# Attention with the divide moved to the output: scores shifted by their row maximum on ScalarE out of PSUM, turned, then exponentiated; the plain block first in the loop

## The chip, the cores and the metric

The kernel runs on one core of a Trainium2 chip. The metric is the device time of one execution in microseconds (us); before the change the median of three runs is 200.62 us. The core's engines are TensorE (PE, with its weight load PEld), VectorE (DVE), ScalarE (ACT), GpSimd (POOL) and SyncE (SP), each with its own instruction queue; they meet at semaphores. All data here is f32.

## The reference, cut to what matters

```python
x = x + conv2d_depthwise(x, 51x51 weights)          # [16, 32, 16, 16]
t = tokens(x)                                       # 16 batches, 256 tokens, 32 channels
# attention over LayerNorm(t), with a mask that also depends on data
scores = where(mask, einsum('bid,bjd->bij', Q, K) * scale, -inf)
w = nan_to_num(softmax(scores, axis=-1))            # 16 x 256 x 256
out = einsum('bij,bjd->bid', w, V) @ Wo + bo        # added to t, then normed per channel group
# 33 steps; in each, the first token's largest channel picks the weights (op) and two flags
def step(h, p):
    op = argmax(h[0, 0, :19])
    attn = softmax(einsum('bqd,bkd->bqk', h @ wq[op], h @ wk[op]) * scale)
    y = einsum('bqk,bkd->bqd', attn, h @ wv[op]) @ wo[op]
    h = where(am[op], y, h)
    z = relu(h @ w1[op] + b1[op]) @ w2[op] + b2[op]
    h = where(fm[op], z, h)
```

Steps whose two flags are both off change nothing and are skipped. With this case's data three steps are left: one with the feed-forward block alone (kind 1, "plain block") and two with attention and feed-forward (kind 3).

## The kernel before, in words

The state is held as hT: 128 partitions (4 batches of 32 channels), 4 groups g of 4 batches, 256 tokens. One run goes: convolution and LayerNorm (to 44 us of the profile); projections and the LIF sweeps on DVE that give the mask (`sweeps`, L1216); the first, masked attention (`attention_pe`, `attention_act`, `attention_dve` with `masked`); a norm (`centred`, `variance`, `scale` on PE, `squared`, `deviation` on ACT, `inverted`, `placed`, `normed` on DVE and POOL); and a loop that each engine runs for itself, on registers read from a table with the picked op (`next_step`). In the loop of before the body is: block A for kinds 2 and 3 (attention), then blocks for kind 1, kind 3 and kind 2. The first pass of this data is of kind 1, so each engine jumps over block A.

Attention goes over 16 batches b, two halves of 128 query rows each. Per batch:

1. PE: scores, 2 products of 128 x 256 (L555). The queries lie in `qz`, where all rows but the batch's 32 are zero, so that a product over all 128 rows gives one batch; 16 copies of 32 x 256 fill it (L981 on ACT; L1050 on ACT and L1412 on DVE in the loop).
2. DVE: the row maximum (L1256; with the mask L1253, which also writes the masked scores to `minus`).
3. ACT: the exponential with the maximum as bias, and the row sum (L905, two of 128 x 256).
4. DVE: the reciprocal of the two sums per row (L1264); POOL: `prob` scaled by it (L448, twice).
5. PE: `turn_pe`, 4 transposes to PSUM (L528); DVE: copy to `probT` (L1269).
6. After every fourth batch PE weighs the values, `weigh_pe` (L542, 8 products of 32 columns), and ACT (in the masked one DVE) drains 128 x 256.

PE's order is fixed: three batches of scores ahead, then per batch scores(b+3), turn(b) and, behind every fourth, the weighing. The last three turns stand in the next block. The feed-forward of kind 3 (`ffn`): token 0's hidden column (L829) and the first batch of hidden products (L813), token 0's row (L834), the last weighing into bank 5 (L843), the second batch of hidden products (it needs group 3 of hT), the outputs (L859), products of the next weights (L772). DVE picks the next op (`pick_op`: L1168, L1158 to L1162); on it SP issues the next weights' DMAs (L419, L420).

Of the kernel before, what the change touches and what calls it, by code (L numbers as in the profile page):

```python
# [6 lines left out]
BF16 = mybir.dt.bfloat16  # L7
# [82 lines left out]
def build(nc, d):  # L90
    with ExitStack() as ctx:
# [11 lines left out]
        def part(t, n):  # L103
# [9 lines left out]
        onesb = sb("onesb", [B, P], BF16)  # L113
        maskc = sb("maskc", [P, NH, S])
# [25 lines left out]
        seen = sb("seen", [1, 1])  # L140

# [12 lines left out]
        qz = sb("qz", [P, B, S])  # L154
        v = sb("v", [P, NH, B, C])
        NPB, NTB = 3, 2 * GB
        prob = [sb(f"prob{i}", [P, NH, S]) for i in range(NPB)]
        relu = big[:, 0:GB * NG * S].rearrange("p (q g s) -> p q g s", q=GB, g=NG)
        probT = [big[:, (GB * NG + NH * i) * S:(GB * NG + NH * (i + 1)) * S].rearrange("p (h s) -> p h s", h=NH)
                 for i in range(NTB)]  # L160
        nmax = sb("nmax", [P, B, NH])
        esum = sb("esum", [P, B, NH])
        einv = sb("einv", [P, B, NH])
        negm = sb("negm", [P, NH, S])
        minus = [sb(f"minus{i}", [P, NH, S]) for i in range(3)]
# [40 lines left out]
        wa = sb("wa", [C, NWA + HID])  # L206
        wf = sb("wf", [HID, C + 2])
        w1r = sb("w1r", [P, HID])
        wfs = sb("wfs", [HID, C + 2])
# [31 lines left out]
        s_S, s_nm, s_P, s_ri, s_Pn, s_T, s_PT = (sem(n) for n in (  # L241
            "scores_in_psum", "row_max_ready", "exponentials_ready", "row_sums_inverted", "probs_ready",
            "probsT_in_psum", "probsT_copied"))
# [4 lines left out]
        s_w1p = sem("first_ffn_rows_placed")  # L248
# [11 lines left out]
        RING = 3  # L260
        SCORES = (0, 1, 4)
        AHEAD = len(SCORES)
# [13 lines left out]
        ATTY = "AAAA"  # L276
        RESY = "DDDD"
        CENTREB = (1, 4, 5, 6)
        VARB = (0, 2, 5, 3)
        LPRE = "ADAD" + "ADAD"  # L280
# [15 lines left out]
        MAIN = B - GB + 1  # L296
        LATTF = LPRE + ATTY[:NG - 1] + FF[:GB] + "A" + FF[GB:]
        K_HF = len(LPRE) + NG - 1
        HBANK = ((0, 1, 4, 2), (5, 6, 3, 7))
        TOKEN0 = bank[7]  # L300
        ZBANK = (1, 4, 2, 5)
        PBANK = (6, 7)
# [4 lines left out]
        class Tasks:  # L307

            def __init__(self, owners, at=0, a=0, d=0):  # L310
                self.owners, self.at, self.a, self.d = owners, at, a, d

            def bank(self, k):
                return bank[8 - RING + k % RING]

# [18 lines left out]
        st = Tasks(STATIC)  # L334
# [104 lines left out]
        def attention_pool(pool, reg_att=None):  # L439
            for b in range(B):  # L440
                if reg_att is None:
                    pool.wait_ge(s_ri, b + 1)
                else:
                    att = pool.snap(reg_att) + 1
                    pool.wait_ge(s_ri, att)
                    pool.reg_alu(reg_att, reg_att, 1, ALU.add)
# [1095 lines left out]
```

## Time and the profile before

| | us |
|---|---|
| median of 3 runs | 200.62 |
| lowest, highest | 198.45, 200.82 |
| span of the profiled execution | 199.1 |
| first products of the two attention rounds start at | 112.73, 153.90 |
| last output stored | 199.1 |

The span runs from the first to the last instruction of the profiled execution. Times below are from its start. The row "PEclk" or the column of that name is the clock granted to TensorE as a share of full speed.

### The profile page before, as it was taken

Reading aid. Unit: us, or ns where it says so; the run is one execution under the profiler, and the core shown is the slowest. Engines: PE = TensorE matmul, PEld = TensorE weight load, DVE = VectorE, ACT = ScalarE, POOL = GpSimd, SP = SyncE. Lnnn points to the kernel's source line nnn. Section 1 sums busy time; section 2 is a strip of 40 time slices with the busy share of each in tenths; the row PEclk is TensorE's granted clock in tenths of the full one; section 3 lists DMA queues with packets and bytes.
Section 4 is the critical chain, followed back from the end, with each engine's and each line's share of the span. In section 5 each row is a group of like instructions: output and inputs, shape, how many; then the busy total and the mean of one; then the engine's idle time right before and its main releaser. Section 6 shows DMA issues by size and latency. Waiting matters only on the chain.

```text
span 199.1 us, 4262 instructions
## 1 busy us (share of the span) xinstructions
PE 166.5 (84%) x1255; PEld 112.6 (57%) x1256; DVE 134.3 (67%) x382; ACT 111.3 (56%) x324; POOL 64.1 (32%) x153
## 2 busy tenths in 40 slices
PE   7999989693898998879929679999867699998770
PEld 5779744241685776647412468776533587775320
DVE  1364578819938889896506388898756689789481
ACT  3464511429767656555405568675655877664670
POOL 8940000100061555453600005655510036556300
PEclk9999999969579999999966999999999999999997
DMA  5900000000000000000000100000000000000003
GB/s 158 315 3 0 3 0 3 0 3 2 0 2 0 2 0 3 0 0 18 3 7 2 20 0 0 0 0 0 0 0 15 0 0 0 0 0 0 0 0 110
DMA packets 3020, 3.33 MB, mean 17 GB/s; under 512 B 889, under 2 KB 2361, under 8 KB 3002
## 3 DMA queue, kind: packets, MB, share of 16 engines
q1 hardware_dynamic: 2858, 2.85, 4.8%
q10 hardware_dynamic: 144, 0.25, 0.4%
q8 instruction: 9, 0.15, 0.3%
q14 instruction: 9, 0.07, 0.1%
HBM read 2.58 MB, written 0.53 MB: 16 GB/s over the span
## 4 chain that ended last, share of the span: by engine, by line
PE 60%; DVE 16%; issue 9%; ACT 8%; POOL 2%; DVEq 1%; ACTq 1%; POOLq 0%
PE bank L555 17%; PE bank L528 8%; PE bank L615 5%; PE bank L542 5%; ACT qz L981 4%; PE bank L679 4%; PE bank L813 3%; PE bank L512 3%; DVE big L1269 3%; PE bank L633 3%; PE bank L600 2%; POOL prob L448 2%; PE bank L694 2%; ACT qz L1050 1%; ACT prob L905 1%
## 5 line engine op out<-in xcount | busy, mean ns | idle before, releaser
L448 POOL TENSOR_SCALAR prob<-prob,einv 128x256 f32<-128x256 f32 x96 | 44.7, 478 | 60.6 <-DVE einv L1264 60.4
L1269 DVE COPY big<-bank 128x512 f32<-128x512 f32 x48 | 32.9, 685 | 5.7 <-PE bank L528 5.7
L905 ACT ACTIVATE prob<-bank,nmax 128x256 f32<-128x256 f32 x64 | 29.8, 473 | 11.6 <-DVE nmax L1256 11.6
L528 PE MATMUL bank<-ident,prob 128*128 128x128 f32 x192 | 30.2, 280 | 6.5 <-POOL prob L448 6.4
L555 PE MATMUL bank<-hT,qz 128*128 128x256 f32 x128 | 32.7, 383 | 0.0
L528 PEld LDWEIGHTS bank<-ident,prob 128*128 128x128 f32 x192 | 21.4, 140 | 18.2 <-POOL prob L448 14.1
L1256 DVE TENSOR_REDUCE nmax<-bank 128x2 f32<-128x512 f32 x32 | 21.6, 687 | 4.8 <-PE bank L555 4.6
L555 PEld LDWEIGHTS bank<-hT,qz 128*128 128x128 f32 x128 | 22.3, 190 | 3.6 <-issue 1.6
L905 ACT ACTIVATE prob<-minus,nmax 128x256 f32<-128x256 f32 x32 | 16.0, 500 | 8.9 <-DVE nmax L1253 7.9
L555 PE MATMUL bank<-kt,qz 128*128 128x256 f32 x64 | 16.5, 386 | 0.9 <-ACT prob L905 0.9
L905 ACT ACTIVATION_READ_ACCUMULATOR prob<-bank,nmax 128x1 f32 x64 | 12.9, 202 | 0.0
L1253 DVE CUSTOM_DVE_ANT_0 minus<-bank,negm 128x256 f32<-128x256 f32 x32 | 11.9, 415 | 1.5 <-PE bank L555 1.5
L555 PEld LDWEIGHTS bank<-kt,qz 128*128 128x128 f32 x64 | 11.1, 190 | 3.2 <-ACT prob L905 1.4
L931 ACT ACTIVATE big<-bank 128x512 f32<-128x512 f32 x14 | 8.2, 598 | 8.2 <-PE bank L615 8.2
L615 PEld LDWEIGHTS bank<-ident,filt 128*128 128x128 f32 x96 | 10.9, 144 | 1.0 <-issue 0.7
L615 PE MATMUL bank<-ident,filt 128*128 128x128 f32 x96 | 11.4, 276 | 0.0
L1106 DVE COPY big<-bank 128x512 f32<-128x512 f32 x10 | 6.8, 686 | 6.6 <-PE bank L615 6.6
L1069 ACT ACTIVATE big<-bank,wfs 128x512 f32<-128x512 f32 x12 | 7.6, 683 | 6.5 <-PE bank L813 6.5
L542 PE MATMUL bank<-big,v 128*32 128x256 f32 x160 | 10.7, 385 | 0.0
L813 PE MATMUL bank<-hT,w1r 32*128 32x512 f32 x48 | 9.7, 800 | 1.1 <-ACT hT L1065 1.1
L1412 DVE COPY qz<-bank 32x256 f32<-32x256 f32 x16 | 6.7, 420 | 5.0 <-PE bank L512 4.9
L595 PE MATMUL bank<-constf,ident 128*128 128x512 bf16 x36 | 8.8, 380 | 0.7 <-DVE xc L1178 0.6
(173 smaller groups left out, 256.8 us busy)
## 6 DMA issues: line engine op xcount, KB each, us to landing
xrev<-xrev_dram SPq DMA_DIRECT2D x1, 512.0 KB, 4.5
xin<-xtok_dram SPq DMA_DIRECT2D x1, 512.0 KB, 5.0
out_dram<-outT SPq DMA_DIRECT2D x2, 256.0 KB, 3.3
maskc<-maskc_dram SPq DMA_DIRECT2D x1, 256.0 KB, 4.8
kx<-kx_dram ACTq DMA_DIRECT2D x1, 248.0 KB, 3.1
wx<-wx_dram SPq DMA_DIRECT2D x1, 216.0 KB, 2.9
constf<-constf_dram SPq DMA_DIRECT2D x1, 186.0 KB, 4.6
wa<-wa_dram SPq DMA_DIRECT2D x3, 56.0 KB, 1.8
```

The costliest lines, as they stand in the source:

```text
L448: last = nc.gpsimd.tensor_scalar(prob[b % NPB][:, ih, :], prob[b % NPB][:, ih, :], einv[:, b, ih:ih + 1], 1.0, ALU.mult, ALU.mult)
L528: mm = pe.transpose(bank[2 + b % 2][:, jh * S + ih * P:jh * S + (ih + 1) * P], prob[b % NPB][:, ih, jh * P:(jh + 1) * P], ident)
L542: mm = pe.matmul(t.bank(k0 + g)[q * C:(q + 1) * C, 0:S], v[:, jh, b, :], probT[b % NTB][:, jh, :], start=(jh == 0), stop=(jh == NH - 1), t ...
L555: mm = pe.matmul(bank[SCORES[b % AHEAD]][:, ih * S:(ih + 1) * S], qz[:, b, ih * P:(ih + 1) * P], keys[:, b // GB, :], start=True, stop=True)
L595: pe.matmul(into, ident[:, 0:P // 2].bitcast(BF16), constf[:, 0:2 * P].bitcast(BF16), start=True, stop=True)
L615: mm = pe.transpose(bank[TBANK[n]][:, u * P:(u + 1) * P], flat(filt[:, ck, a0:a0 + YH, :]), ident)
L813: pe.matmul(bank[HBANK[gp][q]][:, :], w1r[rows, :], flat(hT[rows, 2 * gp:2 * gp + 2, :]), start=True, stop=True, tile_position=(q * C, 0)) ...
L905: e = nc.scalar.activation(prob[b % NPB][:, ih, :], scores, ACT.Exp, bias=nmax[:, b, ih:ih + 1], scale=-1.0 if masked else 1.0, accum_out= ...
L931: nc.scalar.activation(dst, src, ACT.Copy).then_inc(s_toepA, 1)
L1253: m = nc.vector.tensor_tensor_reduce(minus[b % AHEAD][:, ih, :], bank[SCORES[b % AHEAD]][:, ih * S:(ih + 1) * S], negm[:, ih, :], -1.0, -F ...
L1256: m = nc.vector.tensor_reduce(nmax[:, b, :], bank[SCORES[b % AHEAD]][:, :].rearrange("p (h j) -> p h j", h=NH), AX.X, ALU.max, negate=True)
L1269: nc.vector.tensor_copy(flat(probT[b % NTB]), bank[2 + b % 2][:, :]).then_inc(s_PT, 1)
```

## The change: what it does

- **Scores.** `qz` and its zero fill go. The queries are copied as they are, 4 copies of 128 x 256 to `qT` (all on ACT). A batch's scores are products over its own 32 rows (`score_pe`, a row position of the array for each of 4 batches); two batches are issued together, 4 in the front. Score banks are 4, `b % 4`.
- **Exponentials.** In the loop ACT writes scores minus maximum to `sh` (two of 128 x 256, out of PSUM), PE turns that (banks 4 and 5), and ACT takes the exponential of 128 x 512 out of PSUM into `probT`, now 16 tiles. ACT's list is shift(b+4), then exponential(b). In the masked attention DVE writes the masked scores to `sh`, POOL subtracts the maximum, ACT takes the exponential. No row sums on ACT, no reciprocal and no POOL work per batch in the loop, no copy by DVE.
- **Division.** `weigh_pe` gets 8 more products with ones (`onesc`), which leave each batch's sums beside its weighed values; in the masked one also a small product (`tiny`). DVE takes the reciprocal of 128 x 256 and multiplies (`normed_output`), 4 times per attention. In the loop the first two stand in DVE's list behind the row maxima of batches 10 and 14.
- **PE's order.** Per pair n: scores of 2n+4 and 2n+5, turn(2n), for even n the weighing of the group before, turn(2n+1).
- **Masked tail.** All turns now stand ahead; POOL adds the residual of groups 0 and 1, DVE that of 2 and 3 behind its own division.
- **Feed-forward of kind 3.** Outputs of groups 0 and 1 come ahead of the second hidden batch; the latter waits for DVE's division of group 3; DVE's first two relus come ahead of `pick_op`.
- **Loop.** Kind 1 comes first, and its pass falls through to attention. The exponentials' table is asked for once ahead of the loop, not in block A. `w1` moves from the `wa` load to `wf`, repeated for 4 rows groups, and one copy (POOL in the loop) places it.
- **PSUM.** Ring of 2 banks where it was 3, plus two banks for the weighed values; other banks are renumbered.

```diff
+        def score_pe(pe, b, h, keys):
+            g, rows, at_row = strip(b)
+            mm = pe.matmul(bank[b % 4][:, h * S:(h + 1) * S], qT[rows, g, h * P:(h + 1) * P], keys[rows, g, :],
+                           start=True, stop=True, tile_position=at_row)
...
         def weigh_pe(pe, base, t, k0, g):
+            t.drained(pe, k0 + max(g - 1, 0))
...
+            wait(pe, s_P, base, GB * (g + 1))
+            out = bank[YBANKS[g % 2]]
             for jh in range(NH):
                 for q in range(GB):
                     b = g * GB + q
+                    pe.matmul(out[q * C:(q + 1) * C, 0:S], v[:, jh, b, :], probT[b][:, jh, :],
+                              start=(jh == 0), stop=(jh == NH - 1), tile_position=(0, q * C))
+            if t is st:
+                pe.matmul(out[:, S:2 * S], onesq[:, :], tiny[:, :], start=True, stop=False)
+            for jh in range(NH):
+                for q in range(GB):
+                    mm = pe.matmul(out[q * C:(q + 1) * C, S:2 * S], onesc[:, :], probT[g * GB + q][:, jh, :],
+                                   start=t is not st and jh == 0, stop=(jh == NH - 1), tile_position=(0, q * C))
...
+            for n in range(B // 2):
+                if n + 2 < B // 2:
+                    wait(pe, s_nm if masked else s_sh, base, 2 * n + 2)
+                    scores_pe(pe, (2 * n + 4, 2 * n + 5), keys)
+                turn_pe(pe, base, 2 * n)
+                if n % 2 == 0 and n:
+                    weigh_pe(pe, base, t, k0, n // 2 - 1)
+                turn_pe(pe, base, 2 * n + 1)
...
+            def shift_scores(b):
+                wait(act, s_nm, base, b + 1)
+                if b >= NSH:
+                    wait(act, s_T, base, b - NSH + 1)
+                for ih in range(NH):
+                    e = nc.scalar.activation(sh[b % NSH][:, ih, :], bank[b % 4][:, ih * S:(ih + 1) * S], ACT.Identity,
+                                             bias=nmax[:, b, ih:ih + 1])
+                e.then_inc(s_sh, 1)
...
             for b in range(B):
+                if not masked and b + 4 < B:
+                    shift_scores(b + 4)
+                wait(act, s_T, base, b + 1)
+                nc.scalar.activation(flat(probT[b]), bank[4 + b % 2][:, :], ACT.Exp, scale=-1.0 if masked else 1.0).then_inc(s_P, 1)
...
+            def normed_output(t, k, g, to):
+                t.filled(dve, k)
+                link(nc.vector.reciprocal(sinv[:, g, :], bank[YBANKS[g % 2]][:, S:2 * S]))
+                return nc.vector.tensor_tensor(to[:, g, :], bank[YBANKS[g % 2]][:, 0:S], sinv[:, g, :], ALU.mult)
...
+            def attention_dve(base, masked, output, early=()):
+                for b in range(B):
                     row_max(base, b, masked)
+                    if b == 3:
+                        for e in early:
+                            e()
+                    if b in (10, 14):
+                        output((b - 10) // GB)
...
+                def ahead():
+                    product_pe(pe, t, 0, bda[:, :], hT[:, 0, :], S)
+                    product_pe(pe, t, 1, bda[:, :], hT[:, 1, :], S)
+                    t.drained(pe, 1)
+                    scores_pe(pe, (0, 1, 2, 3), hT)
+                    product_pe(pe, t, 2, bda[:, :], hT[:, 2, :], S)
+                    product_pe(pe, t, 3, bda[:, :], hT[:, 3, :], S)
                     for g in range(NG):
                         values(t, NG + g, hT, g, bdv[:, :])
...
+                    token0(r)
+                    hidden(r, 0)
+                    token0_row()
+                    weigh_pe(pe, att, t, len(LPRE), NG - 1)
+                    k = K_HF + GB + 1
+                    t.drained(pe, k - 1)
+                    outputs(t, k, (0, 1))
+                    t.drained(pe, k)
+                    hidden(r, 1)
```

## Rows read from the trace of the kernel before

**Rows 1.** Busy time by stretch: start:end, length, each engine's busy us, PEclk, DMA.

```profile
62.00:91.00 29.00, 25.65 (x173) 17.77 (x171) 25.16 (x115) 17.77 (x66) 14.88 (x32) 1.00 0.00 1
99.50:112.70 13.20, 7.75 (x58) 3.31 (x58) 4.89 (x13) 4.12 (x9) 0.09 (x1) 0.74 0.05 11
121.00:146.00 25.00, 23.01 (x167) 16.65 (x165) 20.48 (x49) 16.71 (x63) 14.60 (x32) 1.00 0.00 0
```

**Rows 2.** Chain that ended last, a loop batch: start, us, scores then turn.

```profile
163.64 0.86 PE bank L555 x4
164.50 0.44 PE bank L528 x4
```

**Rows 3.** Timeline, masked attention, VectorE: start, us, engine, line, operation.

```profile
68.01 0.16 DVE L1263 TENSOR_SCALAR esum<-esum 128x2 f32<-128x2 f32 x1
...
69.56 0.16 DVE L1263 TENSOR_SCALAR esum<-esum 128x2 f32<-128x2 f32 x1
```

**Rows 4.** Groups by line and shape: xcount, busy us, mean ns, idle before.

```profile
L542 PE MATMUL bank<-big,v 128*32 128x256 f32 x160 | 10.7, 385 | 0.0
L1264 DVE RECIPROCAL einv<-esum 128x2 f32<-128x2 f32 x48 | 7.7, 160 | 0.8
L1302 DVE RECIPROCAL invg<-devg 32x32 f32<-32x32 f32 x4 | 1.2, 326 | 1.2 <-ACT devg L1011 1.2
```

**Rows 5.** Timeline, second round's start and feed-forward: instructions back to back.

```profile
147.37 1.26 ACT L1069 ACTIVATE big<-bank,wfs 128x512 f32<-128x512 f32 x2 [0.71 <-PE bank L813]
148.54 1.41 DVE L1441 TENSOR_SCALAR big<-bank,wfs 128x512 f32<-128x512 f32 x2
148.96 1.14 PE L813 MATMUL bank<-hT,w1r 32*128 32x512 f32 x8 [0.55 <-ACT hT L1065]
151.27 0.84 ACT L1075 ACTIVATE hT<-bank,wfs 128x256 f32<-128x256 f32 x2
159.52 1.89 DVE L1256 TENSOR_REDUCE nmax<-bank 128x2 f32<-128x512 f32 x3
```

**Rows 6.** Timeline, VectorE at the start of the masked attention.

```profile
60.02 0.42 DVE L1243 TENSOR_SCALAR spm<-bank 128x256 f32<-128x256 f32 x1 [2.38 <-PE bank L512]
61.21 0.42 DVE L1253 CUSTOM_DVE_ANT_0 minus<-bank,negm 128x256 f32<-128x256 f32 x1
```

**Rows 7.** Timeline, TensorE during the projections: the same two records twice.

```profile
48.05 0.70 PE L512 MATMUL bank<-xt,bdk 128*128 128x256 f32 x2 [1.22 <-ACT qz L981]
49.98 1.22 PE L512 MATMUL bank<-xt,bdk 128*128 128x256 f32 x2 [1.23 <-ACT qz L981]
```

**Rows 8.** Timeline, from the last masked turn to the plain block's first product.

```profile
91.01 0.66 PE L528 MATMUL bank<-ident,prob 128*128 128x128 f32 x4 [0.16 <-POOL prob L448]
94.81 0.70 PE L722 MATMUL bank<-outT,centre 128*128 128x256 f32 x2
99.44 0.42 DVE L1309 TENSOR_TENSOR hT<-bank,hT 128x256 f32<-128x256 f32 x1 [0.79 <-PE bank L736]
103.33 0.34 PE L829 MATMUL bank<-hT,w1r 32*128 32x1 f32 x1 [3.92 <-issue]
```

**Rows 9.** Timeline, plain block: op picked, next weights' DMA, next round's first product.

```profile
106.13 0.18 DVE L1168 COPY row<-bank 1x32 f32<-1x32 f32 x1 [6.27 <-PE bank L835]
107.00 0.14 DVE L1162 TENSOR_SCALAR opi<-top 1x1 int32<-1x1 f32 x1
108.84 0.32 SPq L419 DMA_DIRECT2D wa<-wa_dram  x1
112.73 1.53 PE L512 MATMUL bank<-hT,bda 128*128 128x256 f32 x6 [1.14 <-DVE bdv L1209]
```

**Rows 10.** Timeline, second round: first product of attention, of the feed-forward, row copy.

```profile
153.90 1.56 PE L512 MATMUL bank<-hT,bda 128*128 128x256 f32 x6 [0.57 <-DVE bdv L1209]
187.27 0.27 PE L829 MATMUL bank<-hT,w1r 32*128 32x1 f32 x1
...
188.86 0.18 DVE L1168 COPY row<-bank 1x32 f32<-1x32 f32 x1 [0.79 <-PE bank L835]
```

More of the change, by code:

```diff
@@ L470, in _, with residual, residuals @@
                     nc.gpsimd.tensor_tensor(vg, vg, rep(bvo[:, :], GB), ALU.add).then_inc(s_vb, 1)
-            attention_pool(pool)
+            def residual(g):
+                wait(pool, s_dd, 0, count("D", STATIC[:K_ATT + g + 1]))
+                wait(pool, s_da, 0, count("A", STATIC[:K_ATT]))
+                nc.gpsimd.tensor_tensor(outT[:, g, :], outT[:, g, :], yn[:, g, :], ALU.add).then_inc(s_resP, 1)
+            def residuals(b):
+                if b >= 12 and (b - 12) % 3 == 0:
+                    residual((b - 12) // 3)
+            masked_pool(pool, residuals)
             reg_att = pool.alloc_register("pool_att")
@@ L749, in _ @@
             variance(0)
-            wait(pe, s_PT, 0, B - 1)
             variance(1)
@@ new lines, in hidden, with outputs @@
+                def hidden(r, gp):
+                    for q in range(GB):
+                        rows = slice(q * C, (q + 1) * C)
+                        if (gp, q) == (1, GB - 1):
+                            pe.wait_ge(s_rowc, r)
+                        pe.matmul(bank[HBANK[gp][q]][:, :], w1r[rows, :], flat(hT[rows, 2 * gp:2 * gp + 2, :]),
+                                  start=True, stop=True, tile_position=(q * C, 0)).then_inc(s_task, 1)
+                def outputs(t, k, ns):
+                    for i, n in enumerate(ns):
+                        for q in range(GB):
+                            mm = pe.matmul(bank[ZBANK[n]][q * C:(q + 1) * C, 0:S], w2s, relu[:, q, n, :],
+                                           start=True, stop=True, tile_position=(0, q * C))
+                        mm.then_inc(s_task, 1)
@@ new lines, in outputs @@
+                def outputs(t, k, ns):
+                    for i, n in enumerate(ns):
+                        t.filled(act, k + i)
+                        nc.scalar.activation(hT[:, n, :], bank[ZBANK[n]][:, 0:S], ACT.Identity, bias=b2s).then_inc(s_da, 1)
+                with act.If(kind == 1):
+                    t = Tasks(FF, act.snap(reg_task))
+                    token0(r)
+                    hidden(t, 0, 0)
+                    hidden(t, GB, 1)
+                    outputs(t, 2 * GB, (0, 1, 2))
```

600 lines of the change are left out of this document (268 added, 332 removed).

## The prediction, made before the changed kernel was run

> **What bounds the kernel now.** I read the busy time by stretch first. In the loop's attention (121 to 146 us) TensorE is busy 23.0 of 25.0 us, VectorE 20.5, ScalarE 16.7, at full clock; in the masked one (62 to 91) TensorE 25.7 and VectorE 25.2 of 29 [rows 1]. The chain of work says which of the two it is. In the loop it alternates scores, 0.86, and turn, 0.44, without a gap: 1.30 a batch [rows 2], and a weighing about 1.0 more every fourth (16 records in two passes of the four column strips). In the masked attention VectorE comes round every 1.55 us (68.01 to 69.56) with no idle time in between [rows 3]: it is the bound there. The third place is a hole: hT is ready at 99.44 + 0.42 = 99.86, TensorE starts the plain block at 103.33 after 3.92 us of "issue" [rows 8], and the stretch behind it runs at a mean clock of 0.74 [rows 1].
>
> **Prices.** Turn 0.44; a batch's scores 0.86 over all rows [rows 2]. Hidden products use row strips already: four of 512 columns in 1.14 us, against 4 x 0.86 if they ran one by one (512 columns are twice 256, so 0.86 each) [rows 2, 5]. So strips overlap, and a pair of batches costs 0.86 (0.43 each); if two strips did not overlap, 1.72. Weighing about 1.0 today: 160 records are 10 weighings of 16, four strips at a time [rows 4]; with the ones it doubles, about 2.1. ScalarE: two of 128x512 end in 1.26, two of 128x256 in 0.84, and a single lasts 0.68 and 0.47, so in a row they cost 0.58 and 0.37 [rows 5]. Shift plus exponential: 2 x 0.37 + 0.58 = 1.32 a batch. Row maximum 0.60 in a row, 0.69 alone [rows 5]. POOL's subtraction: as its scaling today, 14.88 / 32 = 0.465, twice a batch [rows 1].
>
> The one operation that is new in kind is VectorE's reciprocal of 128x256. Two elements take 160 ns and 32 take 326 [rows 4], 5.5 ns an element, so 256 take 0.15 + 256 x 0.0055 = 1.55 us. Below that bound stands a plain pass of 256 at 0.42 [rows 6]; above, I allow 2.0. I take 1.55, as both rows are reciprocals. With the multiply 2.0 us a group. The two rows show less than this, and no run here has the length of 256 yet.
>
> **To the masked attention.** `qz`'s copies go, but the mask comes from VectorE's sweeps, which don't change: they end 2.38 us before L1243 at 60.02, which waited for TensorE (busy with scores) [rows 6]. That wait goes; row maxima start near 59.3. The first turn is held by TensorE itself: it now idles some 4 us before the mask, and its clock should be half, as for the record pair of 0.70 that took 1.22 [rows 7]. Transposes of the residual and the spare products then end near 62.4, first turn 63.3.
>
> **Masked attention.** VectorE drops to 0.69 a batch, ScalarE to 0.58, POOL to 0.93; TensorE is the bound: 6 score pairs x 0.86 + 16 turns x 0.44 + 3 weighings x 2.15 = 18.7. Last turn ends at 82.0 instead of 91.67 [rows 8]: -9.7.
>
> **The norm behind it gives much back.** Before, 91.67 to 99.86: 8.2 us. After, from the last turn X: token 0's product and its pick 1.4; division 2 and its residual 2.45 (X+3.85); meanwhile the last weighing and two variances (X+4.7); `centred(2)` 0.6; ScalarE's squares and copies of group 2 and two deviations, which stand behind it, 1.3; two inversions 0.6 (X+7.2); only then division 3, 2.45 (X+9.65). From `centred(3)` on it is as before, 94.81 to 99.86 = 5.05 [rows 8]. X+14.7 = 96.7 instead of 99.86: -3.2.
>
> **Plain block.** Before, 99.86 to 112.73 [rows 8, 9] = 12.9: 3.5 hole, 2.8 to the row copy (at full clock it is 188.86 - 187.27 = 1.6 [rows 10], so 1.2 is slow clock), 2.7 to the DMA, 3.9 to the next product [rows 9]. With the block first, nothing is jumped over; first product to first product then is 9.4 - 1.2 = 8.2: 96.7 + 8.2 = 104.9, -7.8 in all. This needs TensorE's clock up. In the norm it is busy about 0.9 us between X+5 and X+9, less than the share that went before the fall in rows 7 (0.70 in each 1.92); so I let it fall there: +1.5 (spare products, variance, row). -6.3.
>
> **A round's attention,** from its first product (0). Scores of four batches end at 2.2, row maximum 2.9. ScalarE's list mixes 4 shifts with 4 copies, and TensorE's value products wait for these (ring of 2): scores(4) end at 8.35, and exponential 3 at 14.4. From here in groups of four, E3 = end of exponential 3: weighing 2.1 (it waits for E3), turn 5 0.45, scores(10) 1.0, row maximum 0.7: shift 10 at E3+4.4. ScalarE alone would be there at E3+2.6. Division 0 then stands before row maximum 11: +2.0+0.7, shift 11 at E3+7.15; exponential 7 behind it ends at E3+8.5. Before, four batches cost 4 x 1.30 + 1.05 = 6.3. The next group is the same (row maximum 15 behind division 1): E11 = 31.4. The last weighing in the loop 2.1 and turn 13, exponentials 13 and 14: feed-forward at 35.5, against 187.27 - 153.90 = 33.4 [rows 10]. +2.1.
>
> **A round's feed-forward.** Before: second hidden batch 2.9 behind the first (148.96 against 112.73 + 33.4 = 146.1), next product 4.9 behind it [rows 5, 9, 10]. After: VectorE's relu pair 1.4 [rows 5] from +1.3, pick 1.0 (106.13 to 107.14) [rows 9], division 3 from 3.7 to 5.75: second batch at +5.8. +2.9; in the last round +2.5, as the first outputs are added up by then.
>
> **Sum.** -6.3 + (2.1 + 2.9) + (2.1 + 2.5) = +3.3 us. The profiled span is 199.1 and goes to 202.4; the median of runs lies 1.5 above that span, so I add the sum to the median: 203.9. Costed at nothing: `qz`'s zero fill on POOL (TensorE's chain hides it), the table load (ScalarE waits at its place anyhow), the bigger `wf` load and its one copy by POOL (a dozen batches of cover; bare it would be about 0.5).
>
> **Rivals.**
> - *Rounds at ScalarE's pace* (faster): if the weighing and divisions slip into gaps, a batch costs 1.32, 21.1 for 16 where 25 stood: -3.9 instead of +2.1 in each round: -6.3 - 2 x 3.9 + 5.4 = -8.7, 191.9. For it: every engine has room on average. Against: the lists above put the weighing in front of the turns ScalarE needs. 0.08.
> - *The reciprocal costs like a plain pass* (faster): 0.42 instead of 1.55 at the 8 places where it is on the path (2 in the norm, 3 a round): 203.9 - 9.0 = 194.9. It decides from about 0.65 us down. Against: rows 4. 0.17.
> - *TensorE's clock falls inside the rounds* (slower): between exponentials 9 and 11 it does one turn in 4 us. At half clock the weighing, three turns and the hidden batch behind cost 2.8 more, twice: 209.5. For it: rows 7. Against: before, no such gap fell in a round (clock 1.00 [rows 1]). 0.25.
> - *The hole moves*: the second pass now jumps over the plain block; a hole of 3.9 there gives 207.8. Before, the second pass's jump back cost nothing like it (idle 0.57 before 153.90 [rows 10]). 0.05. The Trainium skill ("Runtime: NRT & Kernel Launch", Instruction fetch mechanics) says a taken branch beyond the fetched pages stalls; the trace agrees for 103.33, 3.92 us, and not for 153.90.
>
> **How the numbers follow.** The worked sum has 0.45, with its own range 200 to 207.5 (score pairs, weighing 1.9 to 2.3, reciprocal up to 2.0). The range takes in both a cheap reciprocal and a fallen clock: 194.5 to 209.5. A difference under 2% (4 us) can't be told from none here. Faster by that: the two faster rivals, 0.25. Within: most of the main case, 0.34. Slower: the two slower rivals and a third of the main case, up to 0.41.
>
> **What would show it.** Reciprocal 128x256 at 1.55; masked last turn near 82; hT near 97, the plain block's first product right behind it with no issue gap; round's first product to feed-forward 35.5 with ScalarE waiting on row maxima 10, 11, 14, 15; second hidden batch 5.8 behind the first. It would be wrong if the reciprocal were short, if the weighing were under 1.6, or if TensorE's clock stayed low.

## The result, and the profile after

The changed kernel takes 229.43 us (median of 4 runs, 226.39 to 229.82) against 200.5: 1.141 times the time of before, interval 1.129 to 1.153. Slower was the likeliest sign in the prediction, but 229.4 lies 20 us above the top of its range (194.5 to 209.5). Some runs of every kernel are a few per cent longer, at a lower granted clock: ratios and their 95% intervals are of the fast runs alone, while medians and ranges are of all runs.

The marks of the prediction, in us from the start of each profiled execution. "Predicted" are its numbers on the way to a span of 202.4, its 1.5 us of slow clock in the norm included from the round's first product on. e2, e6 and e4 are experiments described below.

| | before | predicted | after | e2 | e6 | e4 |
|---|---|---|---|---|---|---|
| last masked turn ends | 91.67 | 82.0 | 98.71 | 86.88 | 84.10 | 90.52 |
| plain block's first product | 103.33 | 96.7 | 115.44 | 102.78 | 100.07 | 98.78 |
| round 1's first product | 112.73 | 106.4 | 124.19 | 111.81 | 107.99 | 106.84 |
| round 2's first product | 153.90 | 152.6 | 174.49 | 160.88 | 154.07 | 148.07 |
| end | 199.1 | 202.4 | 227.5 | 214.8 | 203.7 | 192.6 |

After misses by 17.8 us at round 1's first product, by 4.1 more in round 1 (50.3 where 46.2 was predicted) and by 3.2 in round 2 (53.0 against 49.8). Together 25.1, all of the distance from 202.4 to 227.5.

Busy time by stretch of after, columns as in [rows 1]: the masked attention, the norm, the later part of round 1's attention.

```profile
61.40:98.70 37.30, 30.87 (x218) 16.59 (x217) 14.88 (x64) 9.22 (x16) 37.26 (x34) 0.78 0.00 1
98.70:115.70 17.00, 14.16 (x124) 8.35 (x127) 9.26 (x22) 6.52 (x15) 2.50 (x5) 0.70 0.03 8
146.00:158.00 12.00, 7.68 (x68) 4.65 (x72) 4.10 (x6) 6.56 (x16) 0.21 (x1) 0.80 0.01 2
```

In the masked attention GpSimd is busy 37.26 of 37.30 us, where it had 14.88 of 29 before [rows 1]. The chain of work of after says that nothing else counts there (start, us, what):

```profile
61.43 22.68 POOL shifted L448 x21
84.11 0.85 issue
84.96 5.00 POOL shifted L448 x5
...
91.27 6.73 POOL shifted L448 x6
98.00 0.04 issue
98.05 0.66 PE bank L562 x4
```

The groups of after by line and shape, columns as in [rows 4]: the subtraction, the exponential, the reciprocal, and the two halves of the weighing.

```profile
L448 POOL TENSOR_SCALAR shifted<-shifted,nmax 128x256 f32<-128x256 f32 x32 | 35.9, 1142 | 6.4 <-DVE nmax L1314 6.4
L960 ACT ACTIVATE big<-bank 128x512 f32<-128x512 f32 x48 | 28.4, 605 | 40.2 <-PE bank L562 40.2
L1322 DVE RECIPROCAL sinv<-bank 128x256 f32<-128x256 f32 x12 | 20.9, 1745 | 10.1 <-PE bank L582 10.1
L576 PE MATMUL bank<-big,v 128*32 128x256 f32 x192 | 17.0, 484 | 8.7 <-ACT big L960 8.7
L582 PE MATMUL bank<-big,onesc 128*32 128x256 f32 x192 | 16.5, 470 | 0.0
```

A subtraction takes 1142 ns where the scaling on the same engine, with the same shape and the same name of instruction, took 465 ns in a row and 478 as a mean of single records. The weighing's records average 484 ns against 385 [rows 4], which is not a longer product but a lower clock. Round 1 shows where, in its chain of work:

```profile
142.72 1.76 DVE sinv L1322
...
144.88 0.66 DVE nmax L1317
...
146.29 0.61 ACT big L960
146.89 0.14 issue
147.03 1.94 PE bank L576 x16
148.97 1.36 PE bank L582 x16
...
152.61 1.76 DVE sinv L1322
...
156.92 1.94 PE bank L576 x16
158.85 1.53 PE bank L582 x16
```

The reciprocal stands ahead of the row maximum, and the shift and the exponential hang on that. TensorE has nothing in the meantime (2.09 us idle ahead of 147.03 and ahead of 156.92) and then weighs at half clock: the granted clock is 0.50 from 147 to 149 and from 156.9 to 159, and back at 1.00 by 150 and by 160.3. The weighing takes 1.94 + 1.36 and 1.94 + 1.53 us where the same work at full clock takes 1.07 + 0.86 (it did so at 138.50 in this trace). In round 2 the same gap stands ahead of the second and the third weighing, but only the third is slow (1.78 + 2.01 in the timeline, from 207.65). The second has full clock behind a gap as long:

```profile
199.12 1.07 PE L576 MATMUL bank<-big,v 128*32 128x256 f32 x16 [2.09 <-ACT big L960]
```

### The profile page after: what moved, and what is told of

Read it like the earlier page. It is cut to its first block, busy times and chain, and to the rows that moved or that the text cites. A ratio compares the mean times of both kernels' runs of the same rounds, so it can differ in the third digit from the quotient of the medians.

```text
span 227.5 us, 4254 instructions
## 1 busy us (share of the span) xinstructions
PE 178.8 (79%) x1443; PEld 108.1 (48%) x1447; DVE 114.7 (50%) x265; ACT 97.1 (43%) x211; POOL 54.2 (24%) x93
## 4 chain that ended last, share of the span: by engine, by line
PE 40%; DVE 22%; POOL 16%; ACT 9%; issue 9%; DVEq 1%; ACTq 0%; POOLq 0%
POOL shifted L448 15%; PE bank L630 5%; ACT shifted L945 5%; DVE sinv L1322 5%; PE bank L544 4%; PE bank L576 4%; PE bank L582 4%; DVE mem L1276 3%; PE bank L828 3%; ACT big L960 3%; PE bank L648 2%; DVE nmax L1317 2%; PE bank L562 2%; PE bank L835 2%; PE bank L615 2%
## 5 line engine op out<-in xcount | busy, mean ns | idle before, releaser
L960 ACT ACTIVATE big<-bank 128x512 f32<-128x512 f32 x48 | 28.4, 605 | 40.2 <-PE bank L562 40.2
L562 PE MATMUL bank<-ident,shifted 128*128 128x128 f32 x192 | 30.6, 292 | 11.2 <-POOL shifted L448 6.4
L448 POOL TENSOR_SCALAR shifted<-shifted,nmax 128x256 f32<-128x256 f32 x32 | 35.9, 1142 | 6.4 <-DVE nmax L1314 6.4
L945 ACT ACTIVATE shifted<-bank,nmax 128x256 f32<-128x256 f32 x64 | 27.4, 492 | 18.2 <-DVE nmax L1317 18.2
L562 PEld LDWEIGHTS bank<-ident,shifted 128*128 128x128 f32 x192 | 21.4, 147 | 25.3 <-POOL shifted L448 10.6
L1322 DVE RECIPROCAL sinv<-bank 128x256 f32<-128x256 f32 x12 | 20.9, 1745 | 10.1 <-PE bank L582 10.1
L1314 DVE CUSTOM_DVE_ANT_0 shifted<-bank,negm 128x256 f32<-128x256 f32 x32 | 11.6, 420 | 13.6 <-PE bank L544 13.5
L544 PE MATMUL bank<-hT,qT 32*128 32x256 f32 x128 | 16.8, 434 | 0.0
L582 PE MATMUL bank<-big,onesc 128*32 128x256 f32 x192 | 16.5, 470 | 0.0
L544 PEld LDWEIGHTS bank<-hT,qT 32*128 32x128 f32 x128 | 10.1, 201 | 3.8 <-issue 1.7
L980 ACT ACTIVATE big<-bank 128x512 f32<-128x512 f32 x14 | 8.3, 600 | 8.6 <-PE bank L630 8.6
L630 PE MATMUL bank<-ident,filt 128*128 128x128 f32 x96 | 11.8, 282 | 0.0
```

What stands on the lines that cost most here:

```text
L448: last = nc.gpsimd.tensor_scalar(sh[b % NSH][:, ih, :], sh[b % NSH][:, ih, :], nmax[:, b, ih:ih + 1], 1.0, ALU.subtract, ALU.mult)
L544: mm = pe.matmul(bank[b % 4][:, h * S:(h + 1) * S], qT[rows, g, h * P:(h + 1) * P], keys[rows, g, :], start=True, stop=True, tile_position ...
L562: mm = pe.transpose(bank[4 + b % 2][:, jh * S + ih * P:jh * S + (ih + 1) * P], sh[b % NSH][:, ih, jh * P:(jh + 1) * P], ident)
L582: mm = pe.matmul(out[q * C:(q + 1) * C, S:2 * S], onesc[:, :], probT[g * GB + q][:, jh, :], start=t is not st and jh == 0, stop=(jh == NH ...
L630: mm = pe.transpose(bank[TBANK[n]][:, u * P:(u + 1) * P], flat(filt[:, ck, a0:a0 + YH, :]), ident)
L945: e = nc.scalar.activation(sh[b % NSH][:, ih, :], bank[b % 4][:, ih * S:(ih + 1) * S], ACT.Identity, bias=nmax[:, b, ih:ih + 1])
```

## The experiments

In order of what they settle. Each ratio is to runs of before on the same chip. The experiments are spread over four chips, on which the median of before was 200.6 to 201.5, so a difference of 1 us between medians of two experiments means little. Where the text compares stages, it compares the profiled executions, one for each kernel.

### The price of the subtraction: e1_probe, e2_pool_ones, e5_pool_add

Theory A: GpSimd's price depends on the operation. Theory B: on the data (the masked scores hold -1e30). Theory C: GpSimd is slow for a reason in this stage. e1 puts seven instructions at the end of GpSimd's list:

```diff
+            nc.gpsimd.tensor_scalar(scr(0), x256, one, 1.0, ALU.mult, ALU.mult)
+            nc.gpsimd.tensor_scalar(scr(1), x256, one, 1.0, ALU.subtract, ALU.mult)
+            nc.gpsimd.tensor_scalar(scr(2), big30, one, 1.0, ALU.subtract, ALU.mult)
+            nc.gpsimd.tensor_scalar(scr(3), x256, one, 1.0, ALU.add, ALU.mult)
+            nc.gpsimd.tensor_scalar(scr(4), x256, one, 0.0, ALU.mult, ALU.add)
+            nc.gpsimd.tensor_tensor(scr(5), x256, one.broadcast_to([P, S]), ALU.subtract)
+            nc.gpsimd.tensor_tensor(scr(6), x256, one.broadcast_to([P, S]), ALU.mult)
```

> The changed kernel, and behind its loop seven operations of GpSimd on 128x256 f32: multiply-multiply, subtract-multiply (ordinary data, then data with -1e30), add-multiply, multiply-add, and two tensor-tensor forms (subtract, multiply). Their output is used nowhere. Theory A (the pair of operations sets the price): multiply-multiply 0.46 to 0.48 us, subtract-multiply 1.1 us on both data. Rival B (the data sets it): 0.47 on ordinary data and 1.1 on the masked one. Rival C (the place in the masked stage, shared with VectorE, sets it): all about 0.47 here.

The timeline of e1's GpSimd (start, us), in the order of the diff:

```profile
216.23 0.48 POOL L527 TENSOR_SCALAR probe<-xt,onesc 128x256 f32<-128x256 f32 x1 [20.15 <-issue]
216.69 1.15 POOL L528 TENSOR_SCALAR probe<-xt,onesc 128x256 f32<-128x256 f32 x1
217.81 1.15 POOL L529 TENSOR_SCALAR probe<-negm,onesc 128x256 f32<-128x256 f32 x1
218.93 0.48 POOL L530 TENSOR_SCALAR probe<-xt,onesc 128x256 f32<-128x256 f32 x1
219.38 0.48 POOL L531 TENSOR_SCALAR probe<-xt,onesc 128x256 f32<-128x256 f32 x1
219.82 1.05 POOL L532 TENSOR_TENSOR probe<-xt,onesc 128x256 f32<-128x256 f32 x1
220.83 0.61 POOL L533 TENSOR_TENSOR probe<-xt,onesc 128x256 f32<-128x256 f32 x1
```

With `subtract` 1.15, with any of `mult` and `add` 0.48, and the subtraction costs the same on both data. A holds; B and C fall. (e1 as a whole took 227.24 us in its one run.)

e2 replaces the subtraction with a multiply by ones, in place:

```diff
-  nmax[:, b, ih:ih + 1], 1.0, ALU.subtract, ALU.mult)
+  onesc[:, 0:1], 1.0, ALU.mult, ALU.mult)
```

> The changed kernel with GpSimd's subtraction of the row maximum in the masked attention replaced by a multiplication with ones (the same form as the kernel before has; the maximum is left out of these exponentials). If GpSimd's 1.14 us an operation set the masked attention, it falls to 0.47 and the last masked turn comes at about 83 us instead of 98.7, the time at 213 to 215 us. If the price is the place's and not the operation's, nothing changes.

215.98 us (214.05 to 219.25), ratio 1.076 (1.047 to 1.105). The last masked turn ends at 86.88 instead of 98.71, so the subtraction is worth 11.8 us. TensorE then bounds the stage (columns as in [rows 1]):

```profile
64.00:87.00 23.00, 22.32 (x214) 14.10 (x214) 12.89 (x52) 8.49 (x16) 13.67 (x29) 0.98 0.01 2
```

e5 keeps the mathematics: x times -1 plus the maximum, and +1 as the exponential's scale.

```diff
-  nmax[:, b, ih:ih + 1], 1.0, ALU.subtract, ALU.mult)
+  minusone[:, 0:1], nmax[:, b, ih:ih + 1], ALU.mult, ALU.add)
```

> The changed kernel with GpSimd's subtract-multiply written as multiply by -1, then add the maximum (the exponential's sign turned with it): the same results. The multiply-add form measured 0.482 us against 1.145. Expected 214 to 217 us, as with the ones (216.0), last masked turn near 87. Rival: the sign or the pointer in second place brings the slow price back, 229.

214.63 us (213.08 to 219.35), ratio 1.071 (1.057 to 1.084): two operands and another pair of operations are worth 14.8 us of median, 11.9 of it by the last masked turn (86.80). In place the form with two pointer operands takes a little more than the 0.48 of e1:

```profile
L449 POOL TENSOR_SCALAR shifted<-shifted,minusone,nmax 128x256 f32<-128x256 f32 x32 | 17.3, 555 | 12.3 <-DVE nmax L1316 12.3
```

The next kernels build on e5.

### The subtraction elsewhere: e3_masked_act

The masked attention gets the loop's list: ScalarE shifts b+4 (and turns the sign), then exponentiates b; GpSimd subtracts nothing.

```diff
-                if not masked and b + 4 < B:
+                if b + 4 < B:
                     shift_scores(b + 4)
```

> The changed kernel with that subtraction on ScalarE, as in the loop (same results). ScalarE then has 1.32 us a batch, and TensorE 1.4 to 1.5 with the weighing: last masked turn at 84 to 88 us, time 215 to 219 us. If GpSimd was not the bound, no change from 229.

225.82 us (225.77 to 226.21), ratio 1.132 (1.117 to 1.147): 7 us above the top of what was expected. The last masked turn ends at 96.74. The stage now has the loop's trouble: in e3 TensorE's weighings waited 13.3 us for ScalarE over the whole kernel, in after 8.7. In e3's masked attention the reciprocals start at 75.88 and 86.48, ahead of row maxima; TensorE then idles 2.19 and 2.18 us, and the products with ones behind take 1.94 and 1.93 us where 1.07 stood at 72.43.

So ScalarE's busy time, 21.1 of 35 us there, was not the limit; by the trace its shifts wait for row maxima behind a division. No run has e3 with the division moved.

### The division ahead of a row maximum: e6_divide_later, e7_weigh_later, e8_short_reciprocal

e6 is e5 with each division one row maximum later:

```diff
-                    if b in (10, 14):
-                        output((b - 10) // GB)
+                    if b in (11, 15):
+                        output((b - 11) // GB)
```

> The last kernel with VectorE's first two divisions behind the row maxima of batches 11 and 15 instead of 10 and 14. Theory (the division ahead of a row maximum stalls ScalarE's shift and with it the exponential that the weighing waits for): about 1.4 us less per division in the loop, four of them, 5 to 6 us less than without it, so 210 to 211. Rival (the next thing late is TensorE, and the stall moves to the second division or the weighing): under 2 us less.

203.44 us (202.72 to 205.55), ratio 1.016 (1.006 to 1.025): 11.2 less than e5 by medians, twice what was expected, for one exchange. Its chain of work in round 1:

```profile
122.34 1.07 PE bank L578 x16
123.41 0.86 PE bank L584 x16
...
126.56 0.68 DVE nmax L1319
127.24 1.68 DVE sinv L1324
...
128.94 0.44 DVE hT L1325
129.37 1.06 PE bank L578 x16
130.44 0.86 PE bank L584 x16
```

From weighing to weighing 7.03 us, where after has 8.53 (138.50 to 147.03) and then 9.89. The row maximum goes first, ScalarE works beside the reciprocal, and TensorE's clock is still up when the second weighing comes. The third, at 136.39, still has half clock for most of its length (1.45 and 2.01 us for its two halves in the timeline). The weighing's bank is now what it waits for, 0.59 us.

Not all of the 11.2 us is the exchange's. The two rounds take 46.1 + 49.6 = 95.7 us in e6 against 103.0 to 103.3 in e2, after and e7 (below), which have e5's place of the division: some 7.4 us. (e5 itself was profiled in its longest run, with 105.8.) The rest lies ahead of the rounds, where executions differ though the code that runs there is the same: the first masked turn starts at 62.67 in e6, 62.87 in e9 and 62.66 in e10, but at 65.37 in e5 and e8 and 65.46 in e2. In the first three the granted clock is 0.88 or 1.00 from 62 to 63 us, in the others 0.50.

e7 is e5 with the weighing behind both turns of its pair instead of between them:

```diff
-                if n % 2 == 0 and n:
-                    weigh_pe(pe, base, t, k0, n // 2 - 1)
                 turn_pe(pe, base, 2 * n + 1)
+                if n % 2 == 0 and n:
+                    weigh_pe(pe, base, t, k0, n // 2 - 1)
```

> The kernel with the add form, and each weighing behind turn(2n+1) instead of ahead of it. Theory: exponential 2n+1 no longer waits for the weighing, but the next pair's scores still do; 0.5 us less for each of the first two weighings and 2 us for the last one in each round: 4 to 6 us less than without it. Rival: TensorE has to do the weighing anyway before the scores that ScalarE waits for next, so only the last weighing counts: 2 to 3 us less.

215.16 us (214.76 to 215.54), ratio 1.077 (1.067 to 1.087): no gain over 214.63, where 4 to 6 us were expected. TensorE's wait for ScalarE moves from the weighing to the turns (12.3 us ahead of them in e7, 4.9 in e2). The weighing's place is not the cause.

e8 is e6 with the reciprocals of groups 1 to 3 over 32 columns:

```diff
-                link(nc.vector.reciprocal(sinv[:, g, :], bank[YBANKS[g % 2]][:, S:2 * S]))
+                m = S if g == 0 else C
+                link(nc.vector.reciprocal(sinv[:, g, 0:m], bank[YBANKS[g % 2]][:, S:S + m]))
```

> Add form and later divisions (203.4), and the reciprocals of groups 1 to 3 taken over 32 of the 256 columns (the rest of the divisors is left at 1: the division is left out for most tokens of these groups; group 0, from which the next step is picked, is whole). 0.33 us where 1.75 stood. If the reciprocal stands on the path in the norm (two) and ahead of the second hidden batch (one a round) and half of one ahead of the third weighing, 2.8 + 2 x 2.0 = 6.8 us less, 196 to 199. If it is hidden once the order is changed, 202 to 204.

202.21 us (200.62 to 204.72, 10 runs), ratio 1.010 (1.004 to 1.017), only 1.2 below e6, whose interval overlaps. In the profiled executions, which are among the longest of each kernel (204.61 and 205.55 us), the rounds are 3.7 and 1.0 us shorter (42.4 against 46.1, 48.6 against 49.6), where 4.0 was expected. In the norm, where 2.8 was expected, nothing comes back: from the last masked turn to the plain block's first product it is 15.91 us against 15.97. Division 3 is off the path there, or level with another: `centred(3)` starts 9.22 us behind the last turn in e8 and 9.46 in e6, though both reciprocals before it are 1.4 us shorter, because TensorE's spread and variance products, which wait for GpSimd's `invs`, end at about the same time. Round 1 of e8 begins 3.7 later (111.72 against 107.99): 2.7 of it stands at the last masked turn (86.80 against 84.10), from the later start above, and 1.1 comes in the plain block, where the granted clock from 100 to 108 us was 0.50 in e8 and 1.00 in e6. Whether the other nine runs lost the same, the traces don't say. The short reciprocal's group in e8 (the long one's mean there is 1749 ns):

```profile
L1326 DVE RECIPROCAL sinv<-bank 128x32 f32<-128x32 f32 x9 | 3.1, 344 | 8.4 <-PE bank L585 8.4
```

### TensorE's clock: e9_keep_clock, e10_later_and_clock

e9 is e5 with 8 spare products ahead of the waits of the weighings of groups 1 and 2 in the rounds; e10 has the same on e6.

```diff
             out = bank[YBANKS[g % 2]]
+            if t is not st and g in (1, 2):
+                for _ in range(8):
+                    pe.matmul(out, ident[:, 0:P // 2].bitcast(BF16), constf[:, 0:2 * P].bitcast(BF16), start=True, stop=True)
             wait(pe, s_P, base, GB * (g + 1))
```

> The kernel with the add form, and eight spare products (1.7 us at full clock, written into the bank that the weighing overwrites) ahead of the wait of the second and third weighing of each round, where TensorE idled 2.1 us. If the half clock behind these gaps costs 1.5 to 3 us a round, 3 to 5 us less, and the granted clock in the rounds 1.00. If the clock costs nothing there (other waits end last): no change, or 0.5 us more.

208.44 us (three of four runs at 208.4, one at 215.39), ratio 1.042 (1.029 to 1.055), 6.2 below e5 by medians; the clock of 120 to 148 us is 1.00 and the weighing's records take 384 ns:

```profile
120.00:148.00 28.00, 24.98 (x258) 14.87 (x258) 14.57 (x23) 17.30 (x39) 0.44 (x2) 1.00 0.01 2
L581 PE MATMUL bank<-big,v 128*32 128x256 f32 x192 | 12.9, 384 | 1.4 <-ACT big L965 1.4
```

More work for TensorE made the rounds faster: they take 47.3 + 51.1 = 98.4 us against 103.2 in e7 and 103.0 in e2. That is 4.6 to 4.8 us, some 2.4 a round, for the clock behind these gaps. The rest of the 6.2 lies ahead of the rounds, where e9 has no spare products. What falls later stays: from the first hidden batch of round 1 to round 2's first product it is 12.1 us in e9, as in after.

> Add form, later divisions, and the spare products ahead of the second and third weighing of each round. The gaps are shorter here (0.6 us of wait), so the spare products now cost time where there is no gap, and the clock fell only at the last one (records of 2.01 where 1.07 stood): 202 to 204, no gain. Rival: the clock still costs in each round, 200 to 201.

209.81 us (207.86 to 213.55), ratio 1.051 (1.033 to 1.070), 6 us above e6 and above the 202 to 204 expected. Where the gap is only 0.59 us long, the spare products themselves are what the weighing waits for: round 1's second weighing starts 22.4 us into the round instead of 21.4. The two repairs don't add up. But in the profiled executions the rounds are only 1.5 us longer than e6's (97.2 against 95.7), so most of the 6 us is not explained by the traces.

### The plain block first, by itself: e4_before_plain_first

Before, with nothing of the change but the order of the blocks in each engine's loop:

```diff
+                with pe.If(kind == 1):
+                    ffn(...)
+                # the step's code is read again
                 with pe.If(kind >= 2):
                     ...
-                with pe.If(kind == 1):
-                    ffn(...)
```

> The kernel before with one part of the change alone: the plain block first in the loop, falling through to attention. The 3.5 us hole ahead of 103.33 goes, and with it 1.2 us or more of half clock: 195 to 196.5 us. Rival: the hole moves to the second pass, which now jumps over the plain block: 199 to 201.

194.94 us (194.03 to 195.64), ratio 0.977 (0.960 to 0.993): the fastest of all kernels here, just under the 195 to 196.5 expected. The interval lies below 1, though it takes in gains of less than 2%. The timeline of TensorE from the end of the norm, where [rows 8] had 3.92 us of "issue":

```profile
98.78 0.24 PE L813 MATMUL bank<-hT,w1r 32*128 32x1 f32 x1 [0.52 <-issue]
```

The clock in the plain block is 1.00 (99 to 107 us) where it was 0.75 (103 to 113). No hole came up in the second pass, which jumps over the plain block.

### Scores by strip: e11_plain_first_strips, e12_strips_table, e13_strip_pairs, e14_turn_then_pair

e11 is e4 with `qT` and strip products, one batch at a time behind the first three, which are issued together; the attention is otherwise that of before. e12 also asks for the exponentials' table once, ahead of the loop.

```diff
-                    mm = pe.matmul(bank[SCORES[b % AHEAD]][:, ih * S:(ih + 1) * S], qz[:, b, ih * P:(ih + 1) * P],
-                                   keys[:, b // GB, :], start=True, stop=True)
+                    mm = pe.matmul(bank[SCORES[b % AHEAD]][:, ih * S:(ih + 1) * S], qT[rows, g, ih * P:(ih + 1) * P],
+                                   keys[rows, g, :], start=True, stop=True, tile_position=(q * C, 0))
```

> The kernel before with two parts of the change: plain block first, and queries copied whole with scores over each batch's own 32 rows (no zero-filled tile, three batches ahead issued together); softmax order, POOL scaling and copies as before. In each round 16 small copies fall to 4 (3.8 us between first product and scores falls to 1.8) and the first three batches' scores take 1.1 instead of 2.6: -3.5 a round. In the masked attention the mask no longer waits 2.4 us for TensorE: -2. From 194.9 to 185 to 187. Rival (a batch of 32 rows is not faster by itself, and a later engine takes the gain): 190 or more.

199.9 us (197.72 to 201.54, and one of the ten runs at 237.28), ratio 0.999 (0.992 to 1.006), 5 us slower than e4 and 13 above what was expected. TensorE's chain in the loop:

```profile
119.77 0.59 PE bank L527 x4
120.36 1.06 PE bank L559 x4
```

A batch takes 1.65 where it took 1.30 [rows 2]: scores 1.06 for 0.86, turn 0.59 for 0.44.

> The last one, and the exponentials' table asked for once ahead of the loop instead of in each attention block. In each round ScalarE's first query copy waited for 1.5 us of table load and dummy; with the copies short this is on the path: 0.8 to 1 us less a round, 183 to 185. Rival: a load is placed in the block anyhow, no change.

204.64 us (200.44 to 218.14, 11 runs), ratio 1.007 (1.000 to 1.015): no gain in time from the table's place, and some 20 above what was expected, mostly for the reason of e11. The load did leave the block. In round 1 this gives nothing, since in e11 the load (108.62 to 109.90) and its dummy end before ScalarE's first query copy can start: the copy stands 0.7 us behind the round's first product in both. In round 2 the attention is 0.8 us shorter in the profiled executions (33.5 against 34.3).

Why 1.06 and 0.59? The trace of before has the first of them. Its chain, scores (L555) behind a weighing (L542):

```profile
127.75 1.00 PE bank L542 x16
128.75 1.06 PE bank L555 x4
129.81 0.44 PE bank L528 x4
```

In the chain, which counts from end to end, scores over all rows take 0.86 behind a turn of the same shape and 1.06 behind products of another shape. Theory A: each change of shape costs 0.20 ahead of scores and 0.15 ahead of a turn, and strips of two batches run wholly side by side. Theory B: strips overlap only in part. e13 is e11 with scores two batches at a time, halves alternating; e14 has the turn of b ahead of the pair.

```diff
-                if b + AHEAD < B:
-                    scores(b + AHEAD)
+                if b % 2 == 0 and b + AHEAD < B:
+                    scores(*range(b + AHEAD, min(b + AHEAD + 2, B)))
```

> e11_plain_first_strips with scores issued two batches at a time, their strips alternating; look-ahead still 3 banks, so the pair (b+3, b+4) waits for exponential b+1. Theory A (a change of shape between products costs about 0.2 us before scores and 0.15 before a turn, and strips of two batches run wholly side by side): a pair takes 0.86 + 0.20 = 1.06, the turn behind it 0.59, the next turn 0.44, so two batches cost TensorE 2.09 where they cost 3.28. VectorE (row maximum 0.68, reciprocal 0.16, copy about 0.57: 1.4 a batch) is then the bound, against some 1.9 a batch with the weighing in e11: 185 to 192 us in all. Theory B (strips overlap only in part, nothing is paid at a change): the pair takes 1.7 or more, or both turns 0.59, and the time stays within 3 us of e11 (197 to 203).

> As e13_strip_pairs, but turn b stands ahead of the pair (b+3, b+4), so that TensorE has work while it waits for exponential b+1. Theory A: the same records, turns 0.44 before the pair and 0.59 behind it, and a time equal to e13 or up to 4 us less, where e13's trace has TensorE waiting for ScalarE before its pairs. If there is no such wait in e13, this one is slower by up to 3 us, since the scores come a turn later. Theory B: within 3 us of e11.

e13: 199.09 us (196.35 to 202.26), 7 above the range of Theory A in time and within that of Theory B (197 to 203), but its records are those of A. The chain of e13:

```profile
123.18 1.13 PE bank L560 x8
124.31 1.04 PE bank L527 x8
125.39 0.05 issue
125.45 0.66 ACT prob L920 x3
126.11 0.04 issue
126.15 1.13 PE bank L560 x8
```

Two batches' scores take 1.13 (1.06 where no wait stands ahead, as in e14 at 129.62), two turns 1.04, as 0.59 + 0.44 would give. So a pair is 0.86 + 0.20, and two batches cost TensorE 2.1 to 2.2 instead of 3.3. The gain went into a new wait: with three banks for scores the pair waits for exponential b+1, 0.8 us each time. No kernel here has the pairs with four banks and the attention of before. e14 doesn't wait there: 236.56 us (233.33 to 238.24), ratio 1.168 (1.152 to 1.184), with a mean clock of 0.817 over the span, where I had allowed 3 us more than e13. That it brings each score later than ScalarE needs it is my reading; how much of the 37 us is this and how much the clock, no run separates. TensorE waited 29 us for GpSimd ahead of its turns (8.9 in e13) and ran the weighings at 609 ns a record (385 before [rows 4]):

```profile
L541 PE MATMUL bank<-big,v 128*32 128x256 f32 x160 | 18.5, 609 | 0.1
```

## Why the prediction was wrong, by its own steps

**GpSimd's subtraction: the step that failed.** "As its scaling today, 14.88 / 32 = 0.465." I priced an operation that no row showed by its neighbour with the same name, and gave it no second end, though a dearer one would make GpSimd the bound. I put GpSimd at 0.93 a batch and TensorE as the bound, with 18.7 us for the stage. Measured, a subtraction is 1.142; at two a batch GpSimd needs 36.5 us for 16 batches, above every other engine. That is 11.8 of the 25.1 us (e2). Elsewhere ("the reciprocal costs like a plain pass") I did ask what an operation new in kind may cost; here the subtraction passed for an old one.

**Masked attention, the rest: 4.9 us.** e2's last turn ends at 86.88, not 82.0. The first turn comes 2.2 later than 63.3 (65.46): VectorE's first masked scores are at 60.70, not 59.3, and ahead of the turn TensorE runs spare products and a pair of scores at half clock (2.34 and 1.73 us). Other executions had this turn at 62.7, so 63.3 was within reach. From the first turn on it is 21.4 us, not 18.7. Nine turns stand behind a pair or a weighing and cost 0.59 instead of 0.44, 1.4 in all. Five pairs cost 1.06 instead of 0.86: 1.0. TensorE waits twice for ScalarE, 0.7, and three weighings of 2.21 make 0.2. Against this goes 0.9, for my sum has six pairs and one of them stands ahead of the first turn. These are 2.4 of the 2.7. The change of shape was to be read in the trace of before (128.75), and I took 0.86 from the chain's usual place.

**Norm and plain block: 1.1 us more than allowed.** 98.71 to 115.44 is 16.7 against 14.7, with a granted clock of 0.70; the plain block takes 8.75 against 8.2; the 1.5 allowed for the clock is to be taken off. That the norm's sum came this near is in part luck: it ran through divisions 2 and 3, and e8, with both reciprocals 1.4 us shorter, has the same norm. The hole's going was right: it was 3.92 us of "issue" and is 0.52 in e4. The Trainium skill ("Runtime: NRT & Kernel Launch", Instruction fetch mechanics) has taken branches beyond the fetched pages stall; the runs agree for this one and show no such stall where the second pass jumps over the plain block. In the norm of e6 the chain shows 2.48 us of "issue" on GpSimd at 91.89; the timeline names what it waits for, VectorE's inversion at 93.98, which stands behind ScalarE's deviation (93.67) and TensorE's variance products (92.56).

**A round's attention: the working right, the clock on the other side.** Exponential 3 ends at 14.2 behind the first product (predicted 14.4), exponential 7 comes 8.5 later (8.5), exponential 11 9.9 later (8.5), the feed-forward 5.6 later (4.1). The last two are the weighings at half clock, 3.3 and 3.5 us for 2.1, and what runs slowly behind them. The list that I worked through, with the division ahead of row maximum 11, was the kernel's. The rival "TensorE's clock falls inside the rounds" had priced this at 2.8 a round and 0.25, with the hidden batch in it; measured it is 2.7 in round 1's attention, and 2.4 a round is what e9 gives back.

**A round's feed-forward.** The second hidden batch stands 5.96 behind the first (5.8). From there to the next round 6.1 instead of 4.9: outputs 1.93 for 1.07 and the weights' products 1.22 for 0.71, the clock again. With the attention's 2.7 this is all of round 1's 4.1. In round 2 the clock takes its share elsewhere: the round starts at 0.50 (174.5 to 178 us), and its first weighing stands 16.1 us behind its first product where round 1 has 14.3; the next two follow 8.53 apart, as predicted, and from the third, at half clock, to the feed-forward it is 5.6. That is 3.3 too much in the attention, and 14.2 against 14.3 behind it.

**The rivals.** ScalarE's pace was not reached: four batches took 8.5 us and more, not 5.3. A reciprocal at a plain pass's price is refuted: 1.745. The Trainium skill ("VectorE: DVE Perf Modes", the fixed hardware budget) led me to an estimate of 2.2 and my rows to 1.55; the measured value lies between, and 344 ns for 32 elements with 1749 for 256 gives 6.3 ns an element. The hole did not move. The clock was the true one of the four.

**The ledger:** subtraction 11.8, the rest of the masked attention 4.9, norm and plain block 1.1, rounds 4.1 + 3.2, nearly all by the clock: 25.1. The first is shown by e2 and e5, the clock's part in the rounds by the granted clock and, for 4.6 to 4.8 of the 7.3, by e9; the other two are sums read from the traces. That e6 comes out at 203.44, beside the 203.9 predicted, proves nothing: it has another order in the loop, and its parts differ from the predicted ones.

What e6 adds is that my hand-made list told me how the round could be mended. It showed a division of 2 us standing ahead of a row maximum on which shift, exponential and weighing hang. I priced it right (8.5 us for four batches against 6.3) and left it. Exchanging the two gives 1.5 us a group directly, and with the clock some 7.4 for both rounds.

Even with the subtraction and the division mended, dividing at the output doesn't pay here. Before, the reciprocal has two elements a batch, and the scaling was GpSimd's work with room to spare; after, it is 256 elements a group, and eight more products each weighing, in the lists of the two engines that were the bound. The profiled executions of e6 and e4, which share the order of the blocks, say where it is lost: the last masked turn of e6 ends 6.4 us earlier (84.10 against 90.52), but from there to the plain block it takes 15.97 us against 8.26, and the two rounds 95.7 against 85.8. The part of the change that pays is the order of the blocks (e4).

## What to carry to other kernels

Price an instruction by its operation and not by its name and shape, and give both ends to whatever no row shows, above all on an engine that gets two of them a batch. In an in-order queue, put what others hang on (the row maximum) ahead of what only its own engine needs (the division); that exchange was worth 7.4 us in the rounds here. When several edits come together, time the plainest by itself: the block order alone gave 0.977 while the whole gave 1.141.

## What the runs showed of the hardware that I had not expected

- GpSimd, 128x256 in f32: a tensor-scalar with `subtract` 1.15 us, with `mult` and `add` 0.48 (0.555 with two pointer operands, in e5); a tensor-tensor `subtract` 1.05, `mult` 0.61.
- TensorE: scores behind products of another tile shape take 1.06 us instead of 0.86, turns 0.59 instead of 0.44. Two batches in different row strips then cost no more than one.
- Three of four gaps of 2.09 us in TensorE's work in the rounds of after went before 1.4 to 1.6 us of extra time for the weighing behind them (half clock, 1.2 GHz); behind the fourth, at 199.12, the clock was full. Eight spare products in each such gap kept the clock at 1.00 and took 4.6 to 4.8 us off the two rounds.
- VectorE's reciprocal in f32: 1745 ns for 256 elements a partition, 344 ns for 32.
